# Graph attention on one core: the third and fourth key jobs one and two rounds sooner

## The reference

```python
q = ((x @ Wq[l].T + bq[l]) * scaling).reshape(n, H, DH)
k = (x @ Wk[l].T).reshape(n, H, DH)
v = (x @ Wv[l].T).reshape(n, H, DH)
scores = jnp.einsum('ehd,ehd->eh', q[tgt], k[srcidx])
m = jax.ops.segment_max(scores, tgt, num_segments=n)
p = jnp.exp(scores - m[tgt])
s = jax.ops.segment_sum(p, tgt, num_segments=n)
w = p / (s[tgt] + 1e-16)
agg = jax.ops.segment_sum(w[:, :, None] * v[srcidx], tgt, num_segments=n)
attn = agg.reshape(n, D) @ Wo[l].T + bo[l]
```

## Time and profile before

| | |
|---|---|
| median of 3 runs | 1036.1 us (1035.81 to 1040.51) |
| the profiled execution's time | 1038.09 us |
| its span, first to last instruction | 1036.1 us |
| PE busy | 959.2 us, 93% |
| DVE busy | 632.2 us, 61% |
| ACT busy | 494.2 us, 48% |
| POOL busy | 251.0 us, 24% |
| mean granted clock of TensorE | 0.978 |

### The profile page before, as it was taken

One profiled execution on the slowest core, in us unless ns is written; L12 is line 12 of the kernel. 1 busy time (PEld: TensorE's weight loads), 2 busy tenths in 40 slices (PEclk: granted clock), 3 DMA queues, 4 the chain that ended last, 5 costly groups with the idle time before them and its releaser, 6 DMA issues.

```text
span 1036.1 us, 15259 instructions
## 1 busy us (share of the span) xinstructions
PE 959.2 (93%) x5378; PEld 683.1 (66%) x5378; DVE 632.2 (61%) x1087; ACT 494.2 (48%) x767; POOL 251.0 (24%) x138
## 2 busy tenths in 40 slices
PE   6999999999998999999999998999899999989925
PEld 2835545888777787777777776746767776767313
DVE  4675476468777224537776675445476677646395
ACT  1664344555724213327666665213576666641054
POOL 2000000599932051500000047110200000480400
PEclk9999999999999999999999999999999999999967
DMA  9201100000200211135565663111066655811102
GB/s 327 71 0 41 41 1 21 1 1 1 82 1 1 70 53 41 66 138 183 170 188 181 186 216 100 41 41 41 20 195 186 181 172 176 236 57 51 53 1 81
DMA packets 58848, 96.14 MB, mean 93 GB/s; under 512 B 8284, under 2 KB 38172, under 8 KB 58270
## 3 DMA queue, kind: packets, MB, share of 16 engines
q1 hardware_dynamic: 55454, 93.11, 28.4%
q10 hardware_dynamic: 3328, 2.15, 0.7%
HBM read 59.58 MB, written 33.55 MB: 90 GB/s over the span
## 4 chain that ended last, share of the span: by engine, by line
PE 72%; POOL 7%; DVE 7%; issue 6%; ACT 3%; DMA 2%; SPq 1%; DVEq 0%; ACTq 0%; POOLq 0%
PE slots L1798 64%; PE slots L1865 9%; POOL MASK L700 3%; POOL MASK L694 1%; DMA PT<-blocks 1%; POOL KR L699 1%; POOL WL L711 1%; DMA W<-in_wkT 1%; POOL X L731 1%; POOL PT L691 1%; ACT X L1114 1%; DVE Q1L L1516 0%; DVE X L1682 0%; SPq L599 0%; DVE SM L1659 0%
## 5 line engine op out<-in xcount | busy, mean ns | idle before, releaser
L1798 PE MATMUL slots<-PT,XN 128*64 128x256 f32 x1024 | 117.6, 382 | 2.6 <-DMA PT<-blocks 2.5
L1587 DVE CUSTOM_DVE_ANT_0 SM<-slots,MASK 128x1024 f32<-128x1024 f32 x64 | 75.7, 1220 | 68.4 <-PE slots L1798 68.4
L1798 PE MATMUL slots<-KS,QS 64*128 64x512 f32 x768 | 105.6, 406 | 4.6 <-DVE nm L1587 3.5
L1798 PEld LDWEIGHTS slots<-PT,XN 128*64 128x64 f32 x1024 | 72.9, 137 | 44.3 <-issue 14.0
L755 POOL TENSOR_TENSOR QS<-QF,QS 128x512 fp32r<-128x512 f32 x16 | 20.7, 1292 | 311.3 <-ACT QS L1034 311.3
L1798 PEld LDWEIGHTS slots<-KS,QS 64*128 64x128 f32 x768 | 70.2, 184 | 25.1 <-issue 10.4
L801 ACT ACTIVATE PT<-slots 128x1024 f32<-128x1024 f32 x68 | 69.4, 1021 | 31.2 <-PE slots L1865 26.3
L1798 PE MATMUL slots<-PT 128*128 128x512 bf16 (+3 forms) x408 | 80.5, 369 | 2.3 <-ACT PT L801 1.2
L1018 ACT ACTIVATE SM<-SM,nm 128x1024 f32<-128x1024 f32 x64 | 73.3, 1145 | 18.8 <-DVE nm L1587 18.2
L1018 ACT ACTIVATE PT<-PT,nm 128x1024 f32<-128x1024 f32 x64 | 73.3, 1145 | 16.9 <-DVE nm L1587 16.5
L1587 DVE CUSTOM_DVE_ANT_0 PT<-slots,MASK 128x1024 f32<-128x1024 f32 x64 | 75.2, 1211 | 4.1 <-PE slots L1798 3.9
(11 more groups left out here) (403 smaller groups left out, 2194.7 us busy)
## 6 DMA issues: line engine op xcount, KB each, us to landing
blocks<-FL SPq DMA_DIRECT2D x56, 512.0 KB, 3.2
PT<-blocks SPq DMA_DIRECT2D x224, 128.0 KB, 3.4
X<-in_x SPq DMA_DIRECT2D x4, 512.0 KB, 11.8
W<-in_wout SPq DMA_DIRECT2D x2, 1024.0 KB, 6.3
W<-in_gq SPq DMA_DIRECT2D x2, 1024.0 KB, 5.1
W<-in_gk SPq DMA_DIRECT2D x2, 1024.0 KB, 5.2
spill<-X SPq DMA_DIRECT2D x4, 512.0 KB, 2.6
SXR<-XTR SPq DMA_DIRECT2D x1, 2048.0 KB, 8.4
```

Of the source, the lines that this page charges most:

```text
L1587: nc.vector.tensor_tensor_reduce(out=SMs[n % SMB], in0=src, in1=MASK[:, unit(n)[2], :], scale=-1.0, scalar=-0.1 * NO_EDGE, op0=ALU.add, op ...
L1798: return nc.tensor.matmul(o_, lhsT, rhs, start=start, stop=stop)
```

## The change

k2 is listed in the round n = 2 instead of n = 4, and k3 in the round n = 6 instead of n = 8. On PE the order becomes: s2 s3, **k2**, turn 0, s4 s5, turn 2, s6 s7, **k3**, turn 4, s8 s9, turn 6. On DVE k2's subtraction comes ahead of flip 1 (it stood between mask step 5 and flip 3) and k3's ahead of flip 5 (it stood between mask step 9 and flip 7). On ACT both roundings move with them. Both layers use the same list.

```diff
@@ -74,9 +74,9 @@
             order.append(("rsum_bc", m // 16 - 1))
         if n % 8 == 4 and 8 <= n < UNITS - 8:
             order.append(("q", n // 8 + 1))
-        if n == 4:
+        if n == 2:
             order.append(("k", 2))
-        if n == 8:
+        if n == 6:
             order.append(("k", 3))
         if n % 8 == 0 and 16 <= n < UNITS - 16:
             order.append(("k", n // 8 + 2))
```

## The result

The change makes the kernel slower by about half a per cent. Eight runs of it had a median of 1044.4 us (1039.2 to 1047.6), eight of the kernel before 1037.8 us (1035.1 to 1041.6): ratio 1.0063, interval 1.0039 to 1.0086. A second set of twelve against 27 runs gave 1043.9 against 1038.2 us, ratio 1.0046 (1.0030 to 1.0062).

A forecast was written before the change was run, and what follows sets the result against it. TensorE (PE) was taken to bound the kernel, with flip 5 and its transfer starting the first aggregation. Per layer +1.1 us of shift and +1.4 us of clock, doubled to +5.0 on 1036.1, gave 1041.1 us, range 1036.5 to 1042.6.

The forecast's parts named there:

- What ends the stretch: From first score to first aggregation, DVE's flip 5 (unit 5's transposition) and its transfer release the aggregation, not PE.
- DVE's idle time and flip 5: DVE idles 0.82 us before k2's subtraction and 1.0 us before k3's; flip 5 starts 1.39 us later.
- The transfer: Unit 5's write-out and way back: last piece lands in 3.4 us, aggregation +1.1 us a layer, bounds +0.5 to +1.4.
- The fall of the clock: PE's 2.8 us gap before the first aggregation halves its clock in each layer: +1.4 us a layer, bounds 0 to 1.6.
- The time and its range: Whole kernel: 1036.1 us, the median of the runs, plus 5.0 gives 1041.1 us; range 1036.5 to 1042.6.
- the worst case: Whole kernel: the slowest case forecast, the full shift, +6.0 us or 1042.1 us.
- Faster: Rival: PE's first wait sets the pace and k2 fills it, -1.3 us a layer, 1033.5 us; chance 0.06.
- hidden: Rival: DMA engines pace the way back and make up the later start, aggregation as before, 1036.1 us; chance 0.09.
- One fall or none: Rival: clock falls before the first aggregation in one layer, 1039.7 us (chance 0.22), or in none, 1038.3 us (0.13).
- The full shift: Rival: transfer before the aggregation lands no faster, slow clock costs 1.6: 2 x (1.4 + 1.6) = +6.0 us, 1042.1; chance 0.10.
- Later work: Behind the first aggregation: next transfers aren't late and all moves as one with PE, so the loss is not won back.

The follow-up runs named there:

- k3_only: The kernel before with only k3 moved, to round n = 6, and k2 left in round n = 4; 1044.4 us against 1038.1, ratio 1.0044.
- k2_only: The kernel before with only k2 moved, to round n = 2, and k3 left in round n = 8; 1039.2 us against 1038.1, ratio 1.0005.
- flips_first: The change with PE's order kept, but on DVE flip 1 ahead of k2's subtraction and flip 5 ahead of k3's; 1036.0 us against before's 1037.9, ratio 0.9977.
- change_third: The change itself, unaltered, profiled once more; one execution of 1041.7 us.
- filled: The change plus twelve unused matmuls per layer on PE just before the first aggregation; 1039.0 us against before's 1038.1, ratio 1.000.
- filled_again: The kernel of filled run once more, beside the change on the same chip; 1040.2 us against before's 1038.2, ratio 1.0012.
- late_agg: The kernel before, its first aggregation in each layer also waiting for unit 5's way back, nothing reordered; 1051.3 us against 1037.9, ratio 1.0120.

## Why the prediction was right and where it failed

- *What ends the stretch.* Right: the chain still runs over flip 5, its write-out and the way back; k3_only, which puts only k3 ahead of flip 5, has the loss, k2_only has not, and flips_first takes it away with PE's order kept.
- *DVE's idle time and flip 5.* Right to 0.1 us: 0.71 and 1.00 us of idle time for the forecast 0.8 and 1.0, +1.43 us for +1.39.
- *The transfer.* The start of the aggregation was forecast at +1.1 us, by a landing in 3.4 us. Over six layers in three profiles it came at +2.09, +1.01, +1.12, +1.00, +1.33 and +0.86, 1.24 in the mean. The first value, from the landing of 4.22 us, lies above the upper bound of 1.4 that I gave: the bound took 3.65 us as the longest landing, although has one of 5.1.
- *The fall of the clock.* The mechanism was right and commoner than the 3 in 4 assumed: six of six. The size was off: 1.4 us was one slow stretch of 3.1 us; in layer 0 of the first profile the clock stayed down for 5.7 us and more of the aggregation's time and cost 2.76 us. The mean is 1.7. With measured terms the sum is 2 x (1.24 + 1.7) = 5.9 us, ratio 1.0057.
- *The time and its range.* This is the step that failed: the time that the sum starts from, and the room left around it. The forecast was hung on a median of three runs, 1036.1 us, where more runs of the same kernel have 1037.8 to 1038.2. Of the 3.3 us between the forecast 1041.1 and the measured 1044.4, 1.7 come from that start and 0.9 from the two terms above, 2 x (1.24 + 1.7) less 5.0; 0.7 stay open. The prediction had worked out 1043.1 from the profiled execution too, and went by the three runs instead. The range's top was set 0.5 us above the worst case, called "the spread between runs". That spread is 6.5 us over eight runs, and the three times shown (1035.81 to 1040.51) already had 4.7 of it. From the better start the forecast would have been 1042.8, the worst case 1043.8, and the top of an honest range some 1045.
- *The rivals.* "Faster" and "hidden" are refuted: k2's move alone won nothing, and of the shift of flip 5 the transfer gave back at most 0.5 us in a layer (change_third, layer 1: +1.37 became +0.86). "One fall or none" didn't occur in the change's profiles, though it did once in k3_only. "The full shift", +6.0 us, is nearest to the measured terms' 5.9 in number, but by luck: the shift was 1.24 us in the mean, not 1.4, and the falls were dearer than its 1.6. "Later work" was right: behind the aggregation nothing takes up the loss.

What stays open: why the clock held through a gap of 3.78 us in k3_only, and how much the falls elsewhere in the kernel, which come and go between executions, put into each ratio; the kernels filled and filled_again came out 1 to 3 us better than their profiles' stretches say.

## What to carry to other kernels

A wait on the busiest engine isn't worth filling until one has asked what ends the next wait. Here the filler (a key job) had a tail on two other engines, rounding and subtraction, that stood in front of the step on which the next transfer hung; with the step put first in that engine's order the same move wins. And a gap on TensorE in front of a transfer can cost more than its length: before the first aggregation nine of ten gaps over 2.6 us were followed by half clock, for 1.3 to 2.8 us more, so work that can be moved into it pays twice.

## What was not expected of the hardware

The landing of the ways back falls into two groups, and an instruction fetch goes with the slower one. Counted from the write-out of flip 5 to the aggregation, wherever PE waited for it, eleven stretches took 5.5 to 6.1 us and six 6.4 to 6.7 us. In all six of the slow ones, and in none of the fast ones, a packet of 0.02 MB of an instruction queue, q8, lay between the two. The DMA view of the change's first profile, layer 0, 477.05 to 483.60:

```profile
q8 instruction: 1, 0.02, 1.1%
```

One of the fast stretches (flips_first, layer 1, 5.76 us) has a smaller packet of another such queue, so not every fetch goes with a delay. Its DMA view, 757.04 to 762.80:

```profile
q14 instruction: 1, 0.01, 0.8%
```

In the change's second profile it wasn't there and the aggregation came 0.97 us sooner. This is an agreement in seventeen stretches, not a test: no run moved the fetch by itself. If the fetch is the cause, it makes the same wait differ by 0.9 us between executions and layers, and is one reason why one profile is a poor measure of a landing.

The other: on a gap of 3.78 us the clock held, on the seven gaps of 2.61 to 3.67 us it fell every time, as on late_agg's 5.72 and 5.95 us, and where it fell it could stay down twice as long (6.43 us of aggregation) as anywhere in the rows shown of before.
